# Seven block products for an attention's output projection, with their sums made beside the attention

## The chip, the cores and the metric

One core of a Trainium2 chip runs the kernel. The metric is the device time of one execution in microseconds (us), as the median of several. TensorE (PE, with its weight loads as PEld), VectorE (DVE), ScalarE (ACT), GpSimd (POOL) and SyncE (SP, which here only issues transfers) are the five engines. They are synchronised by semaphores.

## What is computed

A cross-attention layer and a small expert layer, both with residuals, on 8 batches of 100 latent rows of width 1024. Cut to what matters:

```python
k, v = kv @ Wk, kv @ Wv                      # 361 context rows and 100 latent rows per batch
q = rms_norm(layernorm(x) @ Wq); k = rms_norm(k)     # 32 query heads, 8 key heads, width 128
out = softmax(q k^T / sqrt(128)) v           # [8, 100, 4096]
x = x + tanh(g0) * (out @ Wo)                # Wo: 4096 x 1024
x = x + tanh(g1) * experts(layernorm(x))     # router, top 2 of 8, rank 16 each
```

Every float32 matrix product is made of three: each operand is split into a high part (ScalarE copies it to the rounded type) and a low part (VectorE subtracts), and TensorE adds hi*hi, hi*lo and lo*hi.

## The kernel before

The work has four stretches. Keys and values come first (to about 640 us) and are stored to DRAM. Then 64 units run, one for each of 8 key heads g and 8 batches b (u = 8g + b), each with four query heads. Unit u has a slot, written out by hand for each engine (`slot`, L931, L1337, L1714): TensorE makes the scores of the four heads, VectorE takes maxima and forms `nm` (`maxima`, L1678), ScalarE the exponentials, VectorE a reciprocal, GpSimd scales the probabilities (`scale`, L738), and in the following slot TensorE turns them (`turn_probs`, L888), ScalarE and VectorE split them (`p_split`, L1297 and L1671), and TensorE multiplies by the values (`values`, L901). Query projections for later units fill TensorE in between, up to unit 54. ScalarE takes a unit's output from the bank and SP stores it (`store_attn`, L568) to `at_d`. GpSimd makes the reciprocal root mean squares of the queries by a power, four columns for each unit (`unit_rms`, L733); `maxima` waits for them.

The output projection is 32 chunks: for each half of the batches (`th`, four batches, 400 columns), each half of the output columns (`nh`) and each key head g, one chunk of 4 heads x 4 banks x 3 matmuls of 128x400. A product of eight chunks (th, nh) sums in banks 0 to 3. The chunks of the first product fill TensorE in slots 56 to 63 in place of query work (`last_slot`, L981: seven half heads per slot; unit 55 has neither and is the `bare_slot`, L966), and the last one is spread through what follows unit 63. The other 24 follow. Each chunk's 1 MB of weights (`wo_raw`) and 0.8 MB of attention outputs (`at_raw`) come from DRAM when the chunk two before has been split (`load_chunk`, L576), are split by ScalarE (`wo_hi`, `at_hi`: L1332, L1335) and VectorE (`wo_lo`, `at_lo`: L1708, L1712) once TensorE has done with the chunk two before, and at the end of a product VectorE and ScalarE copy two banks each (`accumulators`, L1797, L1411), for which TensorE waits.

The feed-forward part of a batch is five steps on TensorE: `turn_out` (L1026), `turn_y`, `low_rank`, `turn_h`, `up`, with `residual` (L1802), `norm`, `route_top` (L1825), `route_gates` (L1836) and `final` on VectorE, and a power on GpSimd. Batches 0 to 3 have theirs beside the 16 chunks of th = 1, one for every four chunks; batches 4 to 7 after the last chunk.

Of the kernel before, what the change touches and what calls it, by code (L numbers as in the profile page):

```python
# [14 lines left out]
P = 128  # L15
B = 8
# [119 lines left out]

def cols(t):
    return min(P, ROWS_M - t * P)


def build(nc, x, ctxT, Wq, Wkv, Wo, AR, BmT, vecs, rows, out):
    with ExitStack() as ctx:
# [11 lines left out]
        at_d = nc.dram_tensor("at_d", [G, B, P, QW], F32).ap()  # L154

# [81 lines left out]
        xr = at("xr", LO, [P, 2, D])  # L237
        ar = at("ar", AOP, [P, C, AE])
        bm = at("bm", LO + 8 * KB, [P, D])
# [108 lines left out]
        wo_used = sem("wo_used")  # L348
        oT_act = sem("oT_act")
# [73 lines left out]

        def split_after(m):

            return 8 * (m + 1) if m < G else 8 * G + 2 * (m + 1 - G)

        def chunk_of(m):

            return m // (2 * G), m // G % 2, m % G  # L430

        @block.sync
        def _(sp):
# [138 lines left out]
            def load_chunk_weights(m):  # L572
                th, nh, g = chunk_of(m)
                sp.dma_start(wo_raw[:, m % 2], Wo[nh, g]).then_inc(wo_in[m % 2], 16)

            def load_chunk(m):  # L576
                th, nh, g = chunk_of(m)
                k = m % 2
                if m >= 2:
                    sp.wait_ge(wo_lo_done, split_after(m - 2))  # L580
                for i in range(2):
                    sp.wait_ge(ao_stored[i], stored(g * B + th * TB + 2 + i))
                if m >= 2:
                    load_chunk_weights(m)
                sp.dma_start(at_raw[k][:], at_d[g, TB * th:TB * th + TB].rearrange("b p q -> p b q")).then_inc(wo_in[k], 16)
# [10 lines left out]
            load_chunk_weights(0)  # L596
            load_chunk_weights(1)

# [6 lines left out]
            for n in range(AHEAD):  # L605
                load_heads(n)
            for u in range(UNITS):
                load_heads(u + AHEAD)
                if OUT0 + 1 <= u:
                    load_chunk(u - OUT0 + 1)  # L610
                if u >= 1:
                    if u + 1 < UNITS:
                        load_kT(u + 1)
                    store_attn(u - 1)
                    if u + 1 < UNITS:
                        load_vv(u + 1)
                if u in (OUT0 - 4, OUT0 - 3):
                    load_chunk(u - OUT0 + 4)
            load_chunk(G + 2)
            store_attn(UNITS - 1)  # L620

            def load_res(t):
                sp.dma_start(xr[0:NQ, t % 2], x[t]).then_inc(xr_in[t % 2], 16)

            def store(t):
                sp.wait_ge(x2_done, 2 * t + 2)
                sp.dma_start(out[t], x2[0:NQ, t % 2]).then_inc(x2_stored[t % 2], 16)

            for m in range(G + 3, 2 * G):
                load_chunk(m)  # L630
                if m == G + 4:
                    sp.dma_start(ar[:], AR).then_inc(ffn_in, 16)
                    sp.dma_start(bm[:], BmT).then_inc(ffn_in, 16)
                if m == G + 5:
                    load_res(0)
                    load_res(1)
            for c in range(2 * G):
                t = c // 4
                load_chunk(2 * G + c)
                if c % 4 == 0 and t >= 1:  # L640
                    sp.wait_ge(x1_done, 2 * t)
                    load_res(t + 1)
                if c % 4 == 3 and t >= 1:
                    store(t - 1)
# [11 lines left out]
        def _(pool):  # L656
# [86 lines left out]

            unit_rms(0)
            for u in range(UNITS):
                if u + 1 < UNITS:
# [10 lines left out]
        def _(pe):  # L757
# [155 lines left out]
            def chunk_head(m, i, half=None):  # L913

                k = m % 2
                if m < G:
# [3 lines left out]
                if m == 0 and i == 0:  # L920
                    pe.wait_ge(ms_done, 2 * G)
                    pe.wait_ge(pT_lo_done, 4 * OUT0)
                for n in range(4) if half is None else (2 * half, 2 * half + 1):
                    mm = three(ps[n][:, 0:TW].rearrange("p (b q) -> p b q", b=TB),
                               wo_hi[:, k, i, n * P:(n + 1) * P], wo_lo[:, k, i, n * P:(n + 1) * P],
                               at_hi[:, k, :, i * NQ:(i + 1) * NQ], at_lo[:, k, :, i * NQ:(i + 1) * NQ],
                               m % G == 0 and i == 0, m % G == G - 1 and i == R - 1)
# [53 lines left out]
            def last_slot(u):  # L981
# [16 lines left out]
                x_(4)  # L998
                values(u - 1, 2)
                turn_probs(u - 1, 3)  # L1000
                x_(5)
# [13 lines left out]
            def chunk(m, between=None):  # L1015
                for i in range(R):
                    chunk_head(m, i)
                    if between and i == R // 2 - 1:
                        between()

            def accumulators_free(th, nh):
                m = 2 * (2 * th + nh)
                pe.wait_ge(oT_dve, m)
                pe.wait_ge(oT_act, m)

            def turn_out(t):  # L1026
                o = out_bank(t)
                if t == 0:
                    accumulators_free(1, 0)
# [4 lines left out]
                for c in range(C):  # L1034
                    if t == TB and c % 4 == 0:
                        accumulators_free(1 + c // 4, 1 - c // 4)
# [37 lines left out]
            accumulators_free(0, 1)  # L1074
            for m in range(G, 2 * G):
# [857 lines left out]
```

## Time and profile before

| | us |
|---|---|
| median of 3 runs | 1725.62 (1725.24 to 1725.96) |
| the profiled execution | 1723.91 |
| its span | 1722.0 |
| TensorE busy | 1685.8 |
| VectorE, ScalarE, GpSimd busy | 1176.2, 879.9, 719.0 |
| mean granted TensorE clock | 0.996 of full speed |
| moved by the transfers | 278.13 MB, 162 GB/s |

The span runs from the first to the last instruction seen by the profiler. Matmuls overlap: the record of one 128x400 matmul is some 350 ns long, while they start 184 ns apart.

### The profile page before, as it was taken

What the parts mean: (1) busy time and instruction counts of PE and PEld (TensorE: products, weight loads), DVE (VectorE), ACT (ScalarE), POOL (GpSimd) and SP (SyncE); (2) the same over time, 40 slices, a digit from 0 to 9 for tenths busy, and PEclk for the clock granted to TensorE, in tenths of its full rate; (3) what the DMA queues carried; (4) which work ended last, traced back from release to release, by engine and by line L of the source; (5) the groups of instructions that cost most, each with busy time, mean ns of one, the idle gap of its engine ahead of it and who ended that gap; (6) DMA issues with size and microseconds to landing.
All of it is one profiled execution on the core that took longest, in us unless ns stands there. A gap on an engine that the chain in (4) does not pass through costs nothing.

```text
span 1722.0 us, 26303 instructions
## 1 busy us (share of the span) xinstructions
PE 1685.8 (98%) x9312; PEld 1508.0 (88%) x9312; DVE 1176.2 (68%) x2074; ACT 879.9 (51%) x1655; POOL 719.0 (42%) x584
## 2 busy tenths in 40 slices
PE   7999999999999999999999999999999999999996
PEld 6788888678888869999999999999998999999994
DVE  7788877677777743777777777777777774445547
ACT  5455544454544422666666666666666664333321
POOL 1454444224434410666666666666665541000000
PEclk9999999999999999999999999999999999999999
DMA  5567778636556564334444334433454664765532
GB/s 195 161 182 234 236 210 246 166 118 188 159 178 155 142 236 140 104 116 122 133 132 123 122 125 132 123 118 119 131 150 133 211 212 158 260 221 200 194 106 68
DMA packets 215654, 278.13 MB, mean 162 GB/s; under 512 B 51956, under 2 KB 187956, under 8 KB 210020
## 3 DMA queue, kind: packets, MB, share of 16 engines
q1 hardware_dynamic: 214948, 269.90, 50.6%
q10 hardware_dynamic: 576, 6.55, 0.9%
q8 instruction: 75, 1.23, 0.3%
q14 instruction: 55, 0.45, 0.1%
HBM read 189.77 MB, written 86.64 MB: 161 GB/s over the span
## 4 chain that ended last, share of the span: by engine, by line
PE 92%; DVE 3%; ACT 2%; issue 1%; DMA 0%; POOL 0%; SPq 0%; DVEq 0%; ACTq 0%; POOLq 0%
PE bank L759 28%; PE bank L761 27%; PE bank L760 27%; PE bank L897 5%; PE bank L864 2%; PE bank L793 1%; PE bank L1060 1%; ACT w_hi L1124 1%; DMA wr<-Wkv 0%; ACT w_hi L1115 0%; DVE w_lo L1488 0%; PE bank L1071 0%; PE bank L801 0%; PE bank L1072 0%; PE bank L1051 0%
## 5 line engine op out<-in xcount | busy, mean ns | idle before, releaser
L741 POOL TENSOR_SCALAR pr<-pr,rr 100x461 f32<-100x461 f32 x256 | 370.2, 1452 | 293.5 <-DVE rr L1696 293.5
L759 PE MATMUL bank<-w_hi,a_hi 128*128 128x512 f32 (+1 forms) x856 | 340.9, 398 | 11.6 <-DVE a_lo L1471 8.9
L761 PE MATMUL bank<-w_hi,a_lo 128*128 128x512 f32 (+1 forms) x856 | 334.9, 391 | 0.0
L760 PE MATMUL bank<-w_lo,a_hi 128*128 128x512 f32 (+1 forms) x856 | 334.4, 391 | 0.0
L1308 ACT ACTIVATE pr<-bank,nm,rq 100x461 f32<-100x461 f32 x256 | 188.7, 737 | 155.8 <-DVE nm L1687 152.7
L1681 DVE TENSOR_REDUCE mx<-bank 100x1 f32<-100x461 f32 x256 | 161.4, 631 | 80.3 <-PE bank L761 75.3
L759 PEld LDWEIGHTS bank<-w_hi,a_hi 128*128 128x128 f32 (+1 forms) x856 | 157.8, 184 | 48.7 <-issue 10.0
L761 PEld LDWEIGHTS bank<-w_hi,a_lo 128*128 128x128 f32 (+1 forms) x856 | 157.7, 184 | 38.2
L759 PE MATMUL bank<-xT_hi,wq_hi 128*128 128x400 f32 x512 | 188.2, 367 | 0.4 <-issue 0.4
L760 PEld LDWEIGHTS bank<-w_lo,a_hi 128*128 128x128 f32 (+1 forms) x856 | 158.0, 185 | 34.8
L759 PE MATMUL bank<-at_hi,wo_hi 128*128 128x400 f32 x512 | 182.6, 357 | 2.8 <-DVE oT L1800 2.8
L761 PE MATMUL bank<-xT_hi,wq_lo 128*128 128x400 f32 x512 | 178.0, 348 | 0.0
L760 PE MATMUL bank<-at_lo,wo_hi 128*128 128x400 f32 x512 | 178.0, 348 | 0.0
L760 PE MATMUL bank<-xT_lo,wq_hi 128*128 128x400 f32 x512 | 177.9, 347 | 0.0
L761 PE MATMUL bank<-at_hi,wo_lo 128*128 128x400 f32 x512 | 177.9, 347 | 0.0
L697 POOL TENSOR_TENSOR msk<-ssk,epst 128x4 f32<-128x4 f32 (+1 forms) x60 | 22.9, 382 | 348.7 <-DVE ssk L1502 348.7
L1299 ACT ACTIVATE pT_hi<-bank 120x400 fp32r<-120x400 f32 (+2 forms) x256 | 127.5, 498 | 58.7 <-PE bank L897 58.5
L1675 DVE TENSOR_TENSOR pT_lo<-bank,pT_hi 120x400 fp32r<-120x400 f32 (+2 forms) x256 | 144.6, 565 | 9.5 <-ACT pT_hi L1299 8.7
L897 PEld LDWEIGHTS bank<-ident,pr 100*120 100x120 f32 (+2 forms) x1024 | 110.1, 148 | 12.4
L1471 DVE TENSOR_TENSOR a_lo<-st,a_hi 128x512 fp32r<-128x512 f32 (+1 forms) x104 | 92.5, 891 | 35.3 <-ACT a_hi L1101 34.8
L897 PE MATMUL bank<-ident,pr 100*120 100x100 f32 (+2 forms) x1024 | 116.4, 253 | 0.0
L752 POOL TENSOR_SCALAR mv<-mv 100x1 f32<-100x1 f32 x8 | 9.7, 1214 | 255.2 <-DVE mv L1815 255.2
(133 smaller groups left out, 3497.7 us busy)
## 6 DMA issues: line engine op xcount, KB each, us to landing
wo_raw<-Wo SPq DMA_DIRECT2D x32, 1024.0 KB, 4.9
kT_d<-kst SPq DMA_DIRECT2D x56, 512.0 KB, 5.4
v_d<-vst SPq DMA_DIRECT2D x56, 512.0 KB
at_raw<-at_d SPq DMA_DIRECT2D x32, 800.0 KB, 7.1
kT<-kT_d SPq DMA_DIRECT2D x64, 361.0 KB, 4.7
kvr<-ctxT SPq DMA_DIRECT2D x44, 512.0 KB, 5.6
wq_raw<-Wq SPq DMA_DIRECT2D x32, 512.0 KB, 5.9
vv<-v_d SPq DMA_DIRECT2D x64, 240.0 KB
```

Source lines behind the costliest of these rows:

```text
L697: pool.tensor_tensor(msk[0:n, m], ssk[0:n, m], epst[0:n], ALU.add).then_inc(msk_done, 1)
L741: pool.tensor_scalar(pr[0:NQ, u % 2, i], pr[0:NQ, u % 2, i], rr[0:NQ, i:i + 1], None, ALU.mult).then_inc(p_done, 1)
L759: pe.matmul(o, lh, rh, start=start, stop=False, skip_group_check=more)
L760: pe.matmul(o, lh, rl, start=False, stop=False, skip_group_check=more)
L761: return pe.matmul(o, ll, rh, start=False, stop=stop, skip_group_check=more)
L864: mm = pe.matmul(o, sq[:, n % 2, bb * NQ:(bb + 1) * NQ], ones[:], start=True, stop=True)
L897: mm = pe.transpose(ps[ptbank(u, t)][0:ROWS[t], i * NQ:(i + 1) * NQ], pr[0:NQ, u % 2, i, OFF[t]:OFF[t] + ROWS[t]], ident[0:NQ, 0:NQ])
L1299: act.activation(pT_hi[0:ROWS[t], t], ps[ptbank(u, t)][0:ROWS[t], 0:QW], ACT.Copy).then_inc(pT_hi_done, 1)
L1308: act.activation(pr[0:NQ, u % 2, i], ps[BS[i % 2]][0:NQ, 0:NK], ACT.Exp, bias=nm[0:NQ, i:i + 1], scale=rq[0:NQ, g, R * b + i:R * b + i + 1 ...
L1471: dve.tensor_tensor(a_lo[:, i % RING, :, 0:n], a_src(i), a_hi[:, i % RING, :, 0:n], ALU.subtract).then_inc(a_lo_done, 1)
L1675: dve.tensor_tensor(pT_lo[0:ROWS[t], t], ps[ptbank(u, t)][0:ROWS[t], 0:QW], pT_hi[0:ROWS[t], t], ALU.subtract).then_inc(pT_lo_done, 1)
L1681: dve.tensor_reduce(mx[0:NQ, i:i + 1], ps[BS[i % 2]][0:NQ, 0:NK], AX.X, ALU.max).then_inc(mx_done, 1)
```

## The change

The projection is done as a Winograd form of Strassen's scheme: rows (batches 0 to 3, 4 to 7), inner dimension (key heads 0 to 3, 4 to 7) and output columns (two halves of 512) are each cut in two, and seven products of a quarter of the inner sums take the place of eight. A product now is four chunks (GQ = 4), 28 in all.

- **Operands.** Three products take plain blocks of the heads (P1, P2, P4) and three plain blocks of the weights (P1, P2, P3); the rest take sums of blocks. Four sums of weights are made on GpSimd beside the units and stored to a DRAM tensor `wt_d`: 16 steps, each a load of four 128x512 blocks (1 MB), four additions and a store (1 MB). S3, the difference of the batch halves for key heads 0 to 3, is made the same way in 16 steps in slots 34 to 51 (`s3_d`). S1, S2 and S4 are made of whole chunks' heads on GpSimd just before the split, four 128x400 additions each, for P5, P6 and P3; S2 is stored (`s2_d`) and loaded again for P3, which takes 2.6 MB per chunk.
- **Order.** P1, P7, then P5 and P6 chunk by chunk in turn, P4, P2, P3. P5 and P4 sum in banks 4 to 7, the others in 0 to 3. P1 and P7 are the chunks beside units 56 to 63. The two copies each of VectorE and ScalarE at the end of P1 are made within slot 60.
- **Results.** The products are added up by VectorE while it empties the banks (four instructions for P6, P4 and P3, two for P2) and by three 128x1600 and one 128x800 additions on GpSimd.
- **Feed-forward.** The batches 4 to 7 come first: their steps stand beside the last 8 chunks (P2, P3), one batch for every two chunks; batch 3's in that order has its routing and two last steps behind the last chunk. Then come the other four.
- **Power.** `unit_rms` makes one power of 16 columns for four units, ahead of the scales of each unit u with u % 4 = 3.
- **SP's order.** The load of the next unit's keys stands first in a slot; transfers of the sums follow, then chunks, the store of the unit before and the values' loads. The chunks' first weights are loaded in slots 53 and 54.

```diff
+CHUNKS = ([(P1, c) for c in range(GQ)] + [(P7, c) for c in range(GQ)] + [(o, c) for c in range(GQ) for o in (P5, P6)] +
+          [(o, c) for o in (P4, P2, P3) for c in range(GQ)])
+WT_OPS = ((2, 3, 2, True), (0, 2, 0, False), (3, 3, 0, True), (1, 1, 0, True))
+WT_STEPS = GQ * R
+for _n in range(4 * WT_STEPS):
+    WT_AT.setdefault(max(-1, (_n - 4) * 6 // 7), []).append(_n)
+S3_AT = 34
+for _t in range(B // 2):
+    for _i, _a in enumerate((0, 2, 3, 4, 5)):
+        FFN_AT.setdefault(4 * _t + _a, []).append((_i, _t))
...
@@ sync
             for n in range(AHEAD):
                 load_heads(n)
+                if n == AHEAD - 2:
+                    load_t(0)
+                    load_t(1)
             for u in range(UNITS):
                 load_heads(u + AHEAD)
+                if 1 <= u < UNITS - 1:
+                    load_kT(u + 1)
+                for n in range(WT_STEPS):
+                    if u == WT_DONE[n] + 1:
+                        store_t(n)
+                    if u == WT_DONE[n] + 2 and n + 2 < WT_STEPS:
+                        load_t(n + 2)
+                if 0 <= u - S3_AT - 2 < S3_STEPS:
+                    store_s3(u - S3_AT - 2)
+                if 0 <= u - S3_AT < S3_STEPS:
+                    load_s3(u - S3_AT)
...
@@ gpsimd
             def unit_rms(u):
                 g, b = u // B, u % B
                 pool.wait_ge(ms_done, 2 * g + b // TB + 1)
-                pool.tensor_tensor(rq[0:NQ, g, R * b:R * b + R], ms[0:NQ, R * b:R * b + R], mhalf[0:NQ, 0:R], ALU.pow).then_inc(rq_done, 1)
+                c = slice(R * b, R * (b + TB))
+                pool.tensor_tensor(rq[0:NQ, g, c], ms[0:NQ, c], mhalf[0:NQ, 0:R * TB], ALU.pow).then_inc(rq_done, 1)
...
+            def chunk_sums(m):
+                o, c = CHUNKS[m]
+                pool.wait_ge(at_in[m % 4], a_loaded(m))
+                if o == P6:
+                    pool.wait_ge(at_sum, summed(m - 1))
+                to, x, y = {P5: (a21[c % 2], a21[c % 2], a22[c % 2]), P6: (a11[c % 2], a21[c % 2], a11[c % 2]),
+                            P3: (at_raw[m % 2], at_raw[m % 2], at_more[:, m % 2])}[o]
+                for b in range(TB):
+                    pool.tensor_tensor(to[:, b], x[:, b], y[:, b], ALU.add if o == P5 else ALU.subtract).then_inc(at_sum, 1)
             unit_rms(0)
+            for i in WT_AT[-1]:
+                weight_sum(i)
             for u in range(UNITS):
-                if u + 1 < UNITS:
+                if u % TB == TB - 1 and u + 1 < UNITS:
                     unit_rms(u + 1)
                 for i in range(R):
                     scale(u, i)
+                for i in WT_AT.get(u, ()):
+                    weight_sum(i)
+                if 0 <= u - S3_AT - 1 < S3_STEPS:
+                    early_sum(u - S3_AT - 1)
+                if u == UNITS - 2:
+                    chunk_sums(FIRST_OF[P5])
+            for m in range(FIRST_OF[P6], LAST_OF[P6] + 1):
+                chunk_sums(m)
+            first, second = (slice(0, C // 2), slice(C // 2, C))
+            pool.wait_ge(oT_dve, 10)
+            pool.wait_ge(oT_act, 6)
+            pool.tensor_tensor(oT_late[:, first], oT_late[:, first], oT_early[:, second], ALU.add).then_inc(mix_done, 1)
+            pool.tensor_tensor(oT_early[:, second], oT_early[:, second], oT_late[:, second], ALU.add).then_inc(mix_done, 1)
+            pool.wait_ge(mix_done, 2)
+            pool.tensor_tensor(oT_late[:, second], oT_late[:, second], oT_late[:, first], ALU.add).then_inc(mix_done, 1)
             for t in range(B):
+                if t == 2:
+                    chunk_sums(FIRST_OF[P3])
+                    chunk_sums(FIRST_OF[P3] + 1)
+                    pool.wait_ge(oT_act, 8)
+                    pool.tensor_tensor(oT_early[:, 2:4], oT_early[:, 2:4], c_tmp[:], ALU.add).then_inc(mix_done, 1)
+                if t == 3:
+                    chunk_sums(FIRST_OF[P3] + 2)
+                    chunk_sums(FIRST_OF[P3] + 3)
...
@@ tensor
+            stages = (turn_out, turn_y, low_rank, turn_h, up)
+            for n in range(4 * GQ):
+                for i in range(2):
+                    chunk_head(TAIL0 + n // 2, n % 2 * 2 + i)
+                for i, t in sorted(FFN_AT.get(n, ())):
+                    stages[i](t)
...
@@ vector
+            def accumulators(o):
+                dve.wait_ge(wo_used, R * (LAST_OF[o] + 1))
+                bank = 4 * (o in UPPER)
+                if o == P6:
+                    dve.wait_ge(oT_act, 2)
+                if o in (P4, P3):
+                    dve.wait_ge(mix_done, 3)
+                for n in (0, 1) if o in (P1, P7, P5, P2) else range(4):
+                    acc = ps[bank + n][:, 0:TW]
...
+                    dve.tensor_tensor(to, acc, oT_early[:, n] if o == P6 else to, ALU.add).then_inc(oT_dve, 1)
...
+            accumulators(P3)
             a, b, c, d = range(TB, B)
-            for do, t in ((residual, a), (final, a - 1), (norm, a), (residual, b), (residual, c), (norm, b), (route, a),
+            for do, t in ((route_top, a - 1), (residual, a), (route_gates, a - 1), (norm, a), (residual, b), (final, a - 1),
+                          (residual, c), (norm, b), (route, a),
```

## Rows read from the trace of the kernel before

**Rows 1.** The page, parts 1 (busy us, share, instructions) and 4 (chain by engine).
```profile
PE 1685.8 (98%) x9312; PEld 1508.0 (88%) x9312; DVE 1176.2 (68%) x2074; ACT 879.9 (51%) x1655; POOL 719.0 (42%) x584
...
PE 92%; DVE 3%; ACT 2%; issue 1%; DMA 0%; POOL 0%; SPq 0%; DVEq 0%; ACTq 0%; POOLq 0%
```

**Rows 2.** Windows: from:to, us, busy PE PEld DVE ACT POOL, PEclk, DMA share, GB/s.
```profile
1315.00:1325.00 10.00, 8.62 (x33) 7.73 (x34) 8.14 (x20) 7.90 (x19) 4.36 (x4) 0.66 0.47 150
1446.00:1518.00 72.00, 71.41 (x387) 70.67 (x386) 33.27 (x18) 27.95 (x19) 0.00 (x0) 1.00 0.64 226
1683.00:1722.00 39.00, 25.30 (x144) 17.70 (x143) 29.13 (x86) 5.56 (x16) 3.41 (x8) 0.92 0.25 75
```

**Rows 3.** Windows: one slot of the attention.
```profile
901.37:912.74 11.37, 11.37 (x74) 10.81 (x73) 8.70 (x20) 7.49 (x16) 7.54 (x5) 1.00 0.36 109
```

**Rows 4.** Timeline of PE: first and last matmul of the second product (384).
```profile
1447.14 0.45 PE L759 MATMUL bank<-at_hi,wo_hi 128*128 128x400 f32 x1 [0.59 <-DVE oT L1800]
...
1517.67 0.34 PE L761 MATMUL bank<-at_hi,wo_lo 128*128 128x400 f32 x1
```

**Rows 5.** Waits of PE: total us, times, longest.
```profile
PE bank L759 <- DVE oT L1800: 2.8, 3, 1.1
```

**Rows 6.** Timelines of DVE and PE in the slot of unit 60.
```profile
1387.96 0.16 DVE L1696 RECIPROCAL rr<-rs 100x1 f32<-100x1 f32 x1 [0.41 <-ACT pr L1308]
...
1388.54 0.43 PE L759 MATMUL bank<-at_hi,wo_hi 128*128 128x400 f32 x1
```

**Rows 7.** Groups by line and form: busy us, mean ns, idle before, releaser.
```profile
L736 POOL TENSOR_TENSOR rq<-ms,mhalf 100x4 f32<-100x4 f32 x64 | 88.0, 1375 | 44.1 <-DVE ms L1645 44.1
...
L1708 DVE TENSOR_TENSOR wo_lo<-wo_raw,wo_hi 128x2048 fp32r<-128x2048 f32 x24 | 54.8, 2282 | 60.3 <-ACT wo_hi L1332 60.3
...
L1712 DVE TENSOR_TENSOR at_lo<-at_raw,at_hi 128x1600 fp32r<-128x1600 f32 x24 | 43.6, 1818 | 0.0
...
L707 POOL TENSOR_TENSOR rstd<-rstd,mhalf 100x1 f32<-100x1 f32 x8 | 4.4, 555 | 0.7
```

**Rows 8.** Timelines of POOL and DVE in the keys' stretch.
```profile
48.91 3.39 POOL L673 TENSOR_TENSOR st<-kvr 128x512 f32<-128x512 f32 x1
...
72.98 1.29 POOL L673 TENSOR_TENSOR st<-kvr 128x512 f32<-128x512 f32 x1
...
73.04 1.77 DVE L1509 TENSOR_TENSOR kn<-cb,rk 128x512 f32<-128x512 f32 x1 [1.48 <-POOL rk L701]
```

**Rows 9.** Timelines of DVE, PE and POOL in a slot.
```profile
899.37 0.16 DVE L1687 SCALAR_TENSOR_TENSOR nm<-mx,rq 100x1 f32<-100x1 f32 x1
899.53 0.57 DVE L1675 TENSOR_TENSOR pT_lo<-bank,pT_hi 121x400 fp32r<-121x400 f32 x1
...
900.90 0.35 PE L759 MATMUL bank<-pT_hi,vv 121*128 121x400 f32 x1
...
908.35 1.83 POOL L736 TENSOR_TENSOR rq<-ms,mhalf 100x4 f32<-100x4 f32 x1
```

**Rows 10.** Timelines of POOL and PE in the first two slots.
```profile
681.53 2.47 POOL L736 TENSOR_TENSOR rq<-ms,mhalf 100x4 f32<-100x4 f32 x2 [44.12 <-DVE ms L1645]
687.20 4.30 POOL L741 TENSOR_SCALAR pr<-pr,rr 100x461 f32<-100x461 f32 x3 [3.21 <-DVE rr L1696]
...
693.72 0.91 PE L897 MATMUL bank<-ident,pr 100*121 100x100 f32 x8
```

**Rows 11.** The page, part 6: transfers, count, KB each, median us to landing.
```profile
wo_raw<-Wo SPq DMA_DIRECT2D x32, 1024.0 KB, 4.9
```

**Rows 12.** Timeline of DVE: copies of a product and the next chunk's last split.
```profile
1518.06 1.06 DVE L1800 COPY oT<-bank 128x400 f32<-128x400 f32 x2 [2.79 <-PE bank L761]
...
1522.99 1.82 DVE L1712 TENSOR_TENSOR at_lo<-at_raw,at_hi 128x1600 fp32r<-128x1600 f32 x1
```

**Rows 13.** Timeline of DVE: first and last instruction of a batch's routing.
```profile
1549.41 0.17 DVE L1827 TENSOR_TENSOR lg<-bank,rowc 100x8 f32<-100x8 f32 x1 [5.37 <-PE bank L1060]
...
1553.73 0.29 DVE L1854 TENSOR_TENSOR hw<-bank,we 100x128 f32<-100x128 f32 x1
```

More of the change, by code:

```diff
@@ L348, in build @@
         wo_used = sem("wo_used")
+        t_in = [sem("t_in0"), sem("t_in1")]
+        t_sum = sem("t_sum")
+        t_stored = [sem("t_stored0"), sem("t_stored1")]
+        at_sum = sem("at_sum")
+        at_in = [sem(f"at_in{i}") for i in range(4)]
+        s3_in = [sem(f"s3_in{i}") for i in range(4)]
+        s3_sum = sem("s3_sum")
+        s3_stored = [sem(f"s3_stored{i}") for i in range(4)]
+        s2_stored = sem("s2_stored")
+        mix_done = sem("mix_done")
         oT_act = sem("oT_act")
@@ L422, in experts_bank, with a_raw, a_loaded, summed @@
             return (2, 6, 4, 0)[t - TB] if t >= TB else 6
+        def a_raw(m):
+            o, c = CHUNKS[m]
+            return a21[c % 2] if o == P5 else a11[c % 2] if o == P6 else at_raw[m % 2][:]
         def split_after(m):
             return 8 * (m + 1) if m < G else 8 * G + 2 * (m + 1 - G)
-        def chunk_of(m):
-            return m // (2 * G), m // G % 2, m % G
+        def a_loaded(m):
+            return 16 * sum(A_LOADS[CHUNKS[n][0]] for n in range(m % 4, m + 1, 4))
+        def summed(m):
+            return R * sum(o in SUMMED for o, c in CHUNKS[:m + 1])
+        def batch_of(t):
+            return (t + TB) % B
         @block.sync
@@ new lines, in load_chunk, with load_s3, store_s3 @@
+            def load_chunk(m):
+                load_weights(m)
+                load_heads_of(m)
+            def load_s3(n):
+                if n >= 4:
+                    sp.wait_ge(s3_stored[n % 4], 16 * (n // 4))
+                for th in range(2):
+                    u = n // TB * B + th * TB + n % TB
+                    sp.wait_ge(ao_stored[u % 2], stored(u))
+                    sp.dma_start(s3b[n % 4][th], at_d[u // B, u % B]).then_inc(s3_in[n % 4], 16)
+            def store_s3(n):
+                sp.wait_ge(s3_sum, n + 1)
+                sp.dma_start(s3_d[n // TB, :, n % TB], s3b[n % 4][0]).then_inc(s3_stored[n % 4], 16)
@@ new lines, in store_s2, with load_t, store_t @@
+            def store_s2(c):
+                sp.wait_ge(at_sum, summed(FIRST_OF[P6] + 2 * c))
+                sp.dma_start(s2_d[c], a11[c % 2]).then_inc(s2_stored, 16)
+            def load_t(n):
+                if n >= 2:
+                    sp.wait_ge(t_stored[n % 2], 16 * (n // 2))
+                sp.dma_start(tb[:, n % 2], Wo.rearrange("n (k c) p r d -> c r p (n k) d", k=2)[n // R, n % R]).then_inc(t_in[n % 2], 16)
+            def store_t(n):
+                sp.wait_ge(t_sum, 4 * n + 4)
+                sp.dma_start(wt_d.rearrange("t c p r d -> c r p t d")[n // R, n % R], tb[:, n % 2]).then_inc(t_stored[n % 2], 16)
@@ L997, in last_slot @@
                 x_(3)
-                x_(4)
+                swap = PARTS * (u - OUT0 - 1) + 4 == 2 * R * FIRST_OF[P7]
+                if not swap:
+                    x_(4)
                 values(u - 1, 2)
                 turn_probs(u - 1, 3)
+                if swap:
+                    x_(4)
                 x_(5)
@@ L1013, in _, with chunk @@
                 values(UNITS - 1, t)
-            def chunk(m, between=None):
+            def chunk(m):
                 for i in range(R):
                     chunk_head(m, i)
[L1018 to L1024, printed above, removed]
             def turn_out(t):
@@ L1894, in route @@
-            def route(t):
-                route_top(t)
-                route_gates(t)
+            accumulators(P4)
+            for n in range(4 * GQ):
+                m = TAIL0 + n // 2 + 1
+                at_last = FFN_AT.get(n - 1, ())
+                if n == 2 * GQ:
+                    accumulators(P2)
+                for i, t in at_last:
+                    if i == 2:
+                        route(t)
+                    if i == 4:
+                        final(t)
+                for i, t in FFN_AT.get(n - 2, ()):
+                    if i == 0:
+                        norm(t)
+                if m < len(CHUNKS):
+                    (chunk_heads if n % 2 else chunk_weights)(m)
+                for i, t in at_last:
+                    if i == 0:
+                        residual(t)
```

319 lines of the change are left out of this document (208 added, 111 removed).

## The prediction

> **What bounds the kernel now.** I read the page's busy times and the chain that ended last first: TensorE is busy 1685.8 of 1722.0 us and the chain runs through it for 92% [rows 1]. So a matmul taken out is worth its full pitch, unless its going uncovers a wait. Next the stretches: the output projection alone (8 chunks, 1446 to 1518 us) has TensorE busy 71.4 of 72 us with VectorE at 33, ScalarE at 28, GpSimd at 0 and 226 GB/s; the closing 39 us, the second half of the feed-forward part, are the one place where TensorE is not full (25.3) and VectorE is (29.1) [rows 2]. In the attention a slot (one unit: scores, softmax, values, and query work between) takes 11.37 us, all of it TensorE; GpSimd is busy 7.5, VectorE 8.7 [rows 3]. So there is room beside TensorE for the additions, and the question is whose turn they come in at.
>
> **Products removed.** 32 chunks become 28, of 48 matmuls each: 192 fewer. From the first matmul of a free projection stretch to its last are 383 pitches in 70.53 us, 0.184 each [rows 4]. 192 x 0.184 = 35.4 us off, all on the path. What the products need besides (splits) shrinks by the same 4 chunks and is hidden.
>
> **Turns of the banks.** Before, three products end with TensorE waiting for their copies, 2.8 us in all [rows 5]. After, P5 and P4 use the upper banks, P6 and P4 cover the copies of P7, P5 and P6, and at P2 to P3 the low-rank matmuls of one batch cover them. 2.8 us off (bounds 0 and 4: each wait also restarts the pipeline). New is P1 to P7 inside slot 60. The four copies come behind the unit's last exponential and reciprocal. That reciprocal is at 1387.96 in a slot of this kind, two copies of 0.57 then end near 1389.2, and the half head that would have followed on TensorE at 1388.54 [rows 6] comes behind the delayed one, near 1390.4: 1.9 us on (0.9 to 3).
>
> **Weights' sums and S3 in the slots.** 64 additions of 128x512 and 16 of 128x400 go to GpSimd, four of the 64 ahead of slot 0, the others one per slot and two in every sixth; from slot 35 to 50 one S3 addition more. An unhindered 128x512 addition takes 1.29 us, so a 128x400 one 1.0. The powers shrink from 64 to 16, one before each four units; a one-column power takes 0.56 and a four-column one 1.38 on the mean [rows 7], so a 16-column one is put at 3 to 5. GpSimd's load per slot goes from 7.5 to 8.1, at most 10 or so, of 11.37: there is room. What costs is order. A GpSimd addition and a VectorE instruction with two SBUF inputs exclude each other: the addition from 72.98 to 74.27 holds the VectorE product begun at 73.04 to 74.81, 1.77 instead of 0.69 us; and an addition begun at 48.91 under a weight split is 3.39 long [rows 8]. The trace agrees here with the Trainium skill, SBUF — State Buffer, Who interferes with whom: the pair of ports is locked for a whole instruction, which speaks against this change's additions. In a slot GpSimd falls free at 908.35 [rows 9]; one addition ends at 909.6, two at 910.9, one behind a query-weight split at 910.5. The small product nm, two SBUF inputs, comes 11.37 after 899.37, at 910.74. Behind it VectorE makes pT_lo, ready at 900.08, for the values at 900.90: 0.85 us of slack [rows 9]. nm is held only where an addition runs at 910.74: the 9 slots with two weights' additions and the 8 odd ones with one and S3's, up to 1.1 us, so at most 0.3 is lost in each. The long power, every fourth slot, can hold the same nm, or the next scales. No row shows the two together; I take half of 17 x 0.3, 2.5 us, since most of the wait fits the slack; bounds 0 and 15 (51 slots x 0.3).
>
> **The first slot.** The power starts at 681.53, the first scale at 687.20 (1.43 each), and the fourth ends just before TensorE's first transposes start, 693.72 [rows 10]. The power (3 us) and four additions (5.2) end near 689.7, so four scales end near 695.5: 1.8 us on (0 to 3).
>
> **Transfers.** Each partial sum is a load and a store of 1 MB, 32 MB in 51 slots, S3 9.6 MB in 16 slots: up to 110 GB/s on top of the 109 of [rows 3]. A weights' chunk lands in 4.9 us [rows 11], and the chip's queue moved 226 GB/s over 72 us without a wait [rows 2]. SP sends the keys ahead of them and the values behind, each with a slot to land. In the last stretch P5 and P6 want 16 MB in 70 us, P3 2.6 MB per chunk of 10 us. Nothing on the path; without that cover a late chunk is TensorE's wait (a rival).
>
> **Sums of heads.** 12 chunks (P5, P6, P3) get four 128x400 additions each on GpSimd, 4.2 us, against 8.8 us of matmuls per chunk. A chunk's split before: the chunk two back ends at 1518.06, and the last of the split ends at 1524.8 [rows 12], 6.7 later, 6.1 without ScalarE's copies ahead of it. w_lo (2.29) and at_lo (1.82) [rows 7] may each wait for one addition, 1.0: 8.1, under 8.8. Covered, thinly. The first P5 chunk is split among the last unit's splits: 0.7 us (0 to 3). P3's sums stand in GpSimd's order behind each batch's square root, which waits for a residual on VectorE; worked through they come 1 us early. I take 0.5 (0 to 5).
>
> **The mixing additions.** Three of 128x1600 start when P6 is added in. By 1.29 x 1600/512 each holds 4.0 us. Counting from the end of P6: VectorE's four adds to 2.3, w_lo to 4.6, mix 1 to 8.6, at_lo to 10.3 where the next chunk was due at 8.8; mix 2 to 14.3, w_lo to 16.4, mix 3 to 20.4, at_lo to 22.1 against 19.2. 1.6 + 2.9 = 4.5 us on (0 to 7; nothing if a long addition lets go in between, or if the order falls better). By the rule of the Trainium skill named above the whole 4.5 stands; if the ports were let go within the addition the sum would be 1698.5.
>
> **The end.** Behind the last product stand four adds on VectorE (2.3) where there were two copies (1.1), and batch 3's routing, which VectorE did before the last product's end: top and gates 0.85 + 1.65 = 2.5 [rows 13]. The closing stretch is VectorE's (29 of 39 us), so both are paid: 3.7, with the waits about 3.8 (2 to 6).
>
> **Sum.** -35.4 - 2.8 + 1.9 + 2.5 + 1.8 + 0.7 + 0.5 + 4.5 + 3.8 = -22.5. The profiled execution took 1723.9 (span 1722.0): 1701.4. It lies 1.7 under the median of the runs, 1725.6: 1703.
>
> **Rivals.**
> - All additions hidden (VectorE and GpSimd happen to alternate well): only the swap and the end cost, -35.4 - 2.8 + 1.9 + 3.8 = -32.5, 1693. For it: the slack everywhere computed; against it: the lock rows. 0.13.
> - The last stretch is short of time: if each of the 12 summed chunks comes 1 us late beyond the 0.5, 11.5 on: 1714.5. For it: 8.1 of 8.8 us, and transfers of 2.6 MB. 0.15.
> - The clock falls. In the bare slot TensorE's waits near 1 us are followed by 0.50 of full speed, 1.2 GHz, for some 6 us; 1315 to 1325 shows 0.66 on the mean, so 3.2 us lost [rows 2]. Two such falls, behind the mix waits and the swap: +6.4, 1709. Against it: the present bank waits of 1.1 us leave the clock at 1.00 in 1446 to 1518. The Trainium skill, TensorE: Matmul & The Clock Gate, What's actually happening, has the clock released by activity and throttled without it; waits of 1 to 3 us do bear on it. 0.05.
> - Slower or no gain: the additions hold nm in all 51 slots [rows 8, 9]. If the additions start later than I place them, nm waits for one whole addition, 1.15 us, and another two-input instruction of the slot (q_lo, before the next scores) for the next: 2 x 1.15 less the slack of 0.85 is 1.45 us, x 51 = 74 in place of 2.5: 1774.5. It decides from 0.49 us per slot on (25/51). Against it: GpSimd falls free 2.4 us before nm. 0.05.
> - The work isn't less (some product is made of more matmuls than I count): the lists give 28 x 48. 0.02, time as before.
>
> **How the numbers follow.** The forecast (1697 to 1709) has 0.60. The range reaches to the hidden case and the late chunks, 1693 to 1714, and leaves out the last two. A measurement of this kernel tells 0.2%, 3.5 us, from no change. Faster: all but the slower rival and the unchanged one, 0.93; same 0.03; slower 0.04.
>
> **What would show it.** 1344 projection matmuls instead of 1536, at 0.184. Slots of 11.37 us on the mean over 0 to 50, or 11.4 to 11.45 by my term, and nm longer than 0.16 us there. TensorE waiting for at_lo twice in P4, 1 to 3 us; for the copies once in slot 60. 45 us from the last product's end to the end of the span instead of 41. Wrong would be: slots of 11.8 and more, waits for at_sum through ScalarE in P5, P6 or P3, a clock under 0.95 outside the bare slot, or no wait at all in P4.

## The result, and the profile after

The changed kernel takes 1716.8 us (median of 4 runs, 1715.7 to 1719.9) against 1725.8 (4 runs, 1725.2 to 1729.3): ratio 0.9948, 95% interval 0.9936 to 0.9960. It is 9.0 us faster where 22.5 were forecast; 1703 was predicted, 1693 to 1714 the range. The profiled execution took 1715.65, its span 1713.8.

The page after, parts 1 and 4 (before: [rows 1]), and groups of the attention's slots, on VectorE from 697 to 1290 us and on GpSimd from 697 to 1265 us (line, shapes, count, busy us, mean ns, idle before):

```profile
PE 1665.8 (97%) x9120; PEld 1475.3 (86%) x9120; DVE 1239.6 (72%) x2078; ACT 865.1 (50%) x1647; POOL 873.9 (51%) x668
...
PE 70%; DVE 18%; issue 4%; ACT 4%; DMA 2%; POOL 0%; DVEq 0%; SPq 0%; ACTq 0%; POOLq 0%
...
L1897 DVE TENSOR_TENSOR q_lo<-q_raw,q_hi 128x400 fp32r<-128x400 f32 x50 | 80.2, 1604 | 12.0 <-ACT q_hi L1519 12.0
L1805 DVE TENSOR_TENSOR wq_lo<-wq_raw,wq_hi 128x1024 fp32r<-128x1024 f32 x25 | 57.7, 2307 | 0.0
...
L912 POOL TENSOR_TENSOR tb<-tb 128x512 f32<-128x512 f32 x58 | 84.0, 1450 | 0.4
L896 POOL TENSOR_TENSOR rq<-ms,mhalf 100x16 f32<-100x16 f32 x12 | 35.2, 2931 | 0.0
```

TensorE has lost 192 matmuls, as announced, but only 20.0 us of busy time where 35.4 were counted. Slots 2 to 50, with the same 3529 matmuls, count as 567.7 us busy where they were 557.1: the records of neighbouring matmuls overlap and cover most of a short wait. The chain of work, which before ran through VectorE for 3%, now does so for 18%, 10 of them by maxima, wq_lo and q_lo. These two splits are the rows to look at: before the change the same groups read

```profile
L1655 DVE TENSOR_TENSOR q_lo<-q_raw,q_hi 128x400 fp32r<-128x400 f32 x52 | 46.8, 901 | 12.6 <-ACT q_hi L1288 12.6
L1563 DVE TENSOR_TENSOR wq_lo<-wq_raw,wq_hi 128x1024 fp32r<-128x1024 f32 x26 | 31.8, 1225 | 1.3
```

so each q_lo has grown by 0.7 us and each wq_lo by 1.1. The end of an odd slot (unit 17) and the start of the next show how, by the timelines of GpSimd, VectorE and TensorE after:

```profile
893.63 1.44 POOL L901 TENSOR_SCALAR pr<-pr,rr 100x461 f32<-100x461 f32 x1 [0.62 <-DVE rr L1938]
895.04 1.49 POOL L912 TENSOR_TENSOR tb<-tb 128x512 f32<-128x512 f32 x1
...
893.80 1.58 DVE L1897 TENSOR_TENSOR q_lo<-q_raw,q_hi 128x400 fp32r<-128x400 f32 x1 [0.26 <-ACT q_hi L1519]
895.31 2.31 DVE L1805 TENSOR_TENSOR wq_lo<-wq_raw,wq_hi 128x1024 fp32r<-128x1024 f32 x1
897.54 0.62 DVE L1923 TENSOR_REDUCE mx<-bank 100x1 f32<-100x461 f32 x1
898.29 0.16 DVE L1929 SCALAR_TENSOR_TENSOR nm<-mx,rq 100x1 f32<-100x1 f32 x1
898.40 0.57 DVE L1917 TENSOR_TENSOR pT_lo<-bank,pT_hi 121x400 fp32r<-121x400 f32 x1
...
899.03 0.45 PE L973 MATMUL bank<-pT_hi,vv 121*128 121x400 f32 x1
```

The addition stands behind the fourth scale, q_lo and wq_lo run beside the two, and wq_lo ends only at 897.62. The maxima of unit 18, whose first scores began at 895.80, start right behind it, 1.74 later; in slot 17 and before the change they start 0.82 to 0.85 after the first scores. nm, pT_lo and the values follow late. TensorE pays for it twice in slot 18: 0.19 us at the values' first matmul (899.03 above), and the rest of the 0.47 in the transposes behind the third head's scores, the fifth of which starts at 900.89, when the next pT_lo has just ended (900.85). These eight transposes after and, in the slot of before that is shown below:

```profile
900.31 1.14 PE L1111 MATMUL bank<-ident,pr 100*120 100x100 f32 x8
...
890.71 0.85 PE L897 MATMUL bank<-ident,pr 100*120 100x100 f32 x8
```

Before the change, VectorE had 0.68 us in hand at that place, and wq_lo and q_lo now want 1.8 more:

```profile
885.32 1.23 DVE L1563 TENSOR_TENSOR wq_lo<-wq_raw,wq_hi 128x1024 fp32r<-128x1024 f32 x1
887.22 0.64 DVE L1681 TENSOR_REDUCE mx<-bank 100x1 f32<-100x461 f32 x1 [0.68 <-PE bank L761]
```
In the slots that end without a wq_lo (here unit 16) VectorE still waits after the change for TensorE:

```profile
882.44 1.58 DVE L1897 TENSOR_TENSOR q_lo<-q_raw,q_hi 128x400 fp32r<-128x400 f32 x1 [0.27 <-ACT q_hi L1519]
885.28 0.64 DVE L1923 TENSOR_REDUCE mx<-bank 100x1 f32<-100x461 f32 x1 [1.26 <-PE bank L975]
```

The windows show the outcome for units 17 and 18 (from:to, us, busy PE PEld DVE ACT POOL, PEclk, DMA share, GB/s), and those of the closing stretch from the last product's last matmul on at the bottom, first after and then before:

```profile
884.43:895.80 11.37, 11.37 (x73) 10.78 (x72) 8.57 (x19) 7.50 (x16) 7.21 (x6) 1.00 0.63 195
895.80:907.62 11.82, 11.74 (x73) 10.71 (x72) 9.67 (x19) 6.44 (x15) 7.10 (x6) 1.00 0.75 230
...
1667.45:1713.80 46.35, 30.66 (x170) 23.13 (x168) 33.44 (x103) 6.12 (x18) 3.46 (x8) 0.87 0.22 63
```
```profile
1681.05:1722.00 40.95, 26.62 (x154) 18.78 (x152) 30.18 (x88) 6.60 (x19) 3.41 (x8) 0.93 0.24 71
```

Taken from the starts of each unit's first scores in both traces, the span's 8.2 us come apart like this: 0.6 on ahead of slot 0 (not the change: that start moves between 684.3 and 687.6 in the runs below), slots 0 and 1 4.7 on, slots 2 to 50 14.4 on (0.45 to 0.6 in most even slots, 0.7 to 0.8 in slots 8, 32, 40, 44 and 46; of the odd slots 0.8 in slot 43, 0.08 in 7 and 31, nothing in the others), slots 51 to 59 0.1, slots 60 to 62 1.5 on, and from slot 63 to the end 29.4 off.

In slots 0 and 1 the TensorE clock has a part. TensorE waits 2.79 us ahead of slot 1's first scores at 695.64 (0.76 at 693.04 before the change), and within this wait, at 694.75, the granted clock falls to 0.50 of full speed, the lower level of 1.2 GHz, until 701.57. Before the change it stays at 1.00 there. The windows after and before:

```profile
694.00:702.00 8.00, 6.36 (x23) 5.81 (x24) 4.90 (x9) 2.02 (x5) 4.56 (x5) 0.57 0.75 207
...
694.00:702.00 8.00, 8.00 (x55) 7.56 (x55) 6.34 (x16) 5.11 (x13) 4.62 (x4) 1.00 0.00 0
```

### The profile page after: what moved, and what is told of

Read it like the earlier page. It is cut to its first block, busy times and chain, and to the rows that moved or that the text cites. A ratio compares the mean times of both kernels' runs of the same rounds, so it can differ in the third digit from the quotient of the medians.

```text
span 1713.8 us, 26112 instructions
## 1 busy us (share of the span) xinstructions
PE 1665.8 (97%) x9120; PEld 1475.3 (86%) x9120; DVE 1239.6 (72%) x2078; ACT 865.1 (50%) x1647; POOL 873.9 (51%) x668
## 4 chain that ended last, share of the span: by engine, by line
PE 70%; DVE 18%; issue 4%; ACT 4%; DMA 2%; POOL 0%; DVEq 0%; SPq 0%; ACTq 0%; POOLq 0%
PE bank L973 21%; PE bank L975 20%; PE bank L974 20%; DVE mx L1923 4%; PE bank L1111 3%; DVE wq_lo L1805 3%; DVE q_lo L1897 3%; PE bank L1078 2%; DVE pT_lo L1917 2%; DMA kT_d<-kst 1%; PE bank L1007 1%; ACT pr L1539 1%; DVE q_raw L1875 1%; DVE nm L1929 1%; DVE wo_lo L1943 1%
## 5 line engine op out<-in xcount | busy, mean ns | idle before, releaser
L973 PE MATMUL bank<-at_hi,wo_hi 128*128 128x400 f32 x448 | 159.9, 357 | 2.9 <-DVE at_lo L1954 2.5
L974 PE MATMUL bank<-at_lo,wo_hi 128*128 128x400 f32 x448 | 155.7, 347 | 0.0
L975 PE MATMUL bank<-at_hi,wo_lo 128*128 128x400 f32 x448 | 155.6, 347 | 0.0
L1111 PE MATMUL bank<-ident,pr 100*120 100x100 f32 (+2 forms) x1024 | 122.3, 255 | 2.3 <-DVE pT_lo L1917 0.4
L1332 ACT ACTIVATE a_hi<-st 128x512 fp32r<-128x512 f32 (+1 forms) x104 | 63.2, 609 | 83.8 <-PE bank L975 73.6
```

The lines of the kernel that those rows point to most:

```text
L973: pe.matmul(o, lh, rh, start=start, stop=False, skip_group_check=more)
L974: pe.matmul(o, lh, rl, start=False, stop=False, skip_group_check=more)
L975: return pe.matmul(o, ll, rh, start=False, stop=stop, skip_group_check=more)
L1111: mm = pe.transpose(ps[ptbank(u, t)][0:ROWS[t], i * NQ:(i + 1) * NQ], pr[0:NQ, u % 2, i, OFF[t]:OFF[t] + ROWS[t]], ident[0:NQ, 0:NQ])
L1332: act.activation(a_hi[:, i % RING, :, 0:cols(k % NT)], a_src(i), ACT.Copy).then_inc(a_hi_done, 1)
```

## The experiments

**My theory:** the additions cost what they do because of where they stand, beside VectorE's q_lo and wq_lo. **The rivals:** their transfers (42 MB beside the slots), their mere amount, and the 16-column powers. Every ratio is against the kernel before; "slots 0-1" and "2-50" are us over before, from the same starts.

| run | median us | ratio, 95% interval | slots 0-1 | slots 2-50 |
|---|---|---|---|---|
| after | 1716.8 | 0.9948 (0.9936-0.9960) | 4.7 | 14.4 |
| e1_one_column | 1699.4 | 0.9841 (0.9823-0.9858) | 0.0 | 0.0 |
| e2_behind_nm | 1709.3 | 0.9901 (0.9884-0.9917) | 0.7 | 9.2 |
| e3_odd_moved | 1704.3 | 0.9865 (0.9848-0.9881) | 3.6 | 1.0 |
| e3b_even_moved | 1722.7 | 0.9978 (0.9968-0.9988) | 3.6 | 19.9 |
| e4_power_per_unit | 1712.8 | 0.9921 (0.9905-0.9938) | 1.7 | 12.4 |
| e5_none_ahead | 1700.4 | 0.9846 (0.9830-0.9863) | 0.8 | 1.1 |
| e6_mix_quarters | 1696.3 | 0.9828 (0.9812-0.9844) | 0.8 | 1.0 |
| e7_mix_column | 1697.8 | 0.9831 (0.9815-0.9848) | 0.8 | 1.1 |
| e8_behind_q_lo | 1703.3 | 0.9862 (0.9846-0.9879) | 3.3 | 1.9 |
| e9_residual_before_final | 1697.3 | 0.9832 (0.9815-0.9848) | 0.8 | 1.1 |
| e10_from_slot_1 | 1696.3 | 0.9831 (0.9813-0.9849) | 0.0 | 0.1 |

**1. Additions of one column**, so that the sums stay unfinished.
```diff
-                pool.tensor_tensor(tb[:, n % 2, to], tb[:, n % 2, a], tb[:, n % 2, b],
+                pool.tensor_tensor(tb[:, n % 2, to, 0:1], tb[:, n % 2, a, 0:1], tb[:, n % 2, b, 0:1],
```
and early_sum alike.

> The 64 weights' additions and the 16 early additions of S3 work on one column instead of 512 or 400; all their waits and all 42 MB of their transfers stay, so the products P7, P5, P6 and P4 come out of unfinished sums. Theory (an addition queued directly behind the fourth scale holds q_lo, 1.58 instead of 0.90 us, and wq_lo, 2.31 instead of 1.22, and the next slot's first maxima come late): q_lo back to 0.90, wq_lo to 1.22, slots 2 to 50 back to 11.37 on the mean (-14 us), the first two slots nearly back (-4): 1697 to 1700 against 1716. Rival (the transfers beside the slots delay loads or slow SBUF): no change, 1714 to 1718, q_lo and wq_lo as long as now.

1699.4. q_lo and wq_lo are back to 901 and 1225 ns, and every slot up to 50 has its old length:

```profile
L1897 DVE TENSOR_TENSOR q_lo<-q_raw,q_hi 128x400 fp32r<-128x400 f32 x50 | 45.1, 901 | 12.1 <-ACT q_hi L1519 12.1
L1805 DVE TENSOR_TENSOR wq_lo<-wq_raw,wq_hi 128x1024 fp32r<-128x1024 f32 x25 | 30.6, 1225 | 1.2
```

All transfers and all the long powers are still there. So the transfers beside the slots cost nothing there, and neither do the powers by themselves.

**2. All additions behind a slot's first nm.** The pool's loop, with END_AT empty here, GAP_AT spreading the 64 over slots 0 to 50:
```diff
-            for i in WT_AT[-1]:
-                weight_sum(i)
...
+                if u in GAP_AT or u in S3_GAP:
+                    pool.wait_ge(nm_done, 4 * u + 1)
+                for i in GAP_AT.get(u, ()):
+                    weight_sum(i)
+                for n in S3_GAP.get(u, ()):
+                    early_sum(n)
                 for i in range(R):
                     scale(u, i)
```

> Full additions, but each stands in GpSimd's order in front of a slot's first scale, behind a wait for the slot's first nm, where GpSimd idles for 3.2 us (885.2 to 888.35) and VectorE reads banks; at most two per slot, none ahead of slot 0. Theory: q_lo and wq_lo are free again, slots 2 to 50 take 11.37 to 11.45, and the first slots are shorter: 1697 to 1703. In the slots with two additions the first scale comes up to 0.8 us late, which I expect to be hidden. Rival (it is the amount of additions, wherever they stand, or their transfers): 1712 to 1717, with nm, pT_lo or q_raw longer instead.

1709.3, a miss against 1697 to 1703. q_lo is back at 0.90, and from slot 2 on the slots with one addition behind nm have their old length; but those with two are 0.13 to 0.6 longer. The timelines of GpSimd and VectorE in such a slot:

```profile
893.16 2.65 POOL L915 TENSOR_TENSOR tb<-tb 128x512 f32<-128x512 f32 x2 [2.57 <-DVE nm L1938]
...
894.84 0.99 DVE L1938 SCALAR_TENSOR_TENSOR nm<-mx,rq 100x1 f32<-100x1 f32 x1
```

The second addition holds the second nm, 0.99 instead of 0.16, and the exponentials wait. My expectation had the late scale in it and not this. So there is room for one addition there, not for two.

**3. Only one parity moved.** In the run e3_odd_moved the additions at the ends of odd slots went behind the next nm, in its mirror those at the ends of even slots:
```diff
+    _u = max(-1, (_n - 4) * 6 // 7)
+    _move = _u % 2 == 1 and _u > 0
+    (GAP_AT if _move else END_AT).setdefault(_u + _move, []).append(_n)
```

> Only the additions behind the last scale of the odd slots (those in which wq_lo is made) move behind the next slot's first nm; those of the even slots and the four ahead of slot 0 stay. Theory (the loss is wq_lo's, 0.47 us in each even slot because VectorE has 1.26 us of slack at the other slots' ends): nearly all 14 us of slots 2 to 50 come back, 1701 to 1705, with q_lo still 1.58 in the even slots. Rival (every held q_lo costs its share): half of it, 1708 to 1711.

> The mirror of the run that moved the odd slots' additions: now those behind the last scale of the even slots move behind the next slot's first nm, and those beside wq_lo in the odd slots stay. Theory (the loss is wq_lo's alone): the even slots keep their 0.47 us, nothing is gained, and the slots with two additions behind nm lose 0.4 more: 1716 to 1722. Rival (every addition behind a fourth scale costs a share): 1709 to 1712.

1704.3 and 1722.7. Moving the odd half gives back 13.4 of the 14.4 us, with q_lo still held in the even slots (mean 1242 over all). Moving the even half gives nothing and costs 5.5, in the odd slots that now have two additions behind nm; I had allowed for less of this, and the time lies just above my 1716 to 1722. An addition beside q_lo alone is free, since VectorE waits 1.26 us for TensorE behind it; two cost at most 0.08 (slots 7 and 31). Three, at the end of slot 42, with a 16-column power behind them, cost 0.8 in slot 43: GpSimd is done with them only at 1192.87, makes its four scales without a pause until 1198.58, and q_lo beside them takes 2.58 us. Beside wq_lo even one addition costs 0.47.

**4. A power per unit.**
```diff
-                if u % TB == TB - 1 and u + 1 < UNITS:
+                if u + 1 < UNITS:
                     unit_rms(u + 1)
```
with four columns each, and VectorE's waits for rq_done as before the change.

> One four-column power per unit as before the change, instead of one of 16 columns for four units; all else is as after. Theory (the 2.9 us power is hidden, since the slots with it are no longer than the others): the first slot gains up to 1.5 us from the shorter first power, the rest stays or loses where the power, now 1 to 1.5 us in every slot behind the addition, runs at the first nm: 1714 to 1722. Rival (the long power is what makes slots late): 1705 to 1711.

1712.8, between the two: 3.1 us come from slots 0 and 1 (I had allowed 1.5), 2.0 from slots 2 to 50. Together with e1_one_column, where the long powers cost nothing, the long power is harmless by itself and costs something where additions are queued with it. The traces tell where: the 2.0 us are those of slots 7 and 8, 31 and 32, 43 and 44, and 0.15 in slot 40. In slots 7, 31 and 43 the 16-column power stands directly behind two or three additions; it does so in slot 19 too, and there costs nothing.

**5. No additions ahead of slot 0** (on top of e3_odd_moved): `_u = _n * 4 // 5`.

> As the run that moved the odd slots' additions, and no weights' addition ahead of slot 0: the 64 stand evenly in slots 0 to 50. Theory (the four additions, 5.2 us, push the first four scales and with them everything in slots 0 and 1): slots 0 and 1 take 9.0 and 11.4 instead of 11.0 and 13.0 us, 3.6 off, 1700 to 1702. Rival (the 16-column power of 2.9 us is what delays the first slot): less than 1 us off, 1703 to 1705.

1700.4, in the range of the theory; but slots 0 and 1 gain 2.8, not 3.6: they take 9.7 and 11.6 us and still lose 0.8. Not all of the 2.8 is the scales' delay. TensorE's clock was granted at 0.50 for 3.4 us of slot 1 in e3_odd_moved (13.0 us) and for 6.8 us in the changed kernel (14.1 us), and stayed at 1.00 in e5_none_ahead (11.6 us). These runs do not separate the clock's part from the rest.

**6. The mixing additions** in quarters and, in another run, of one column (both on top of e5_none_ahead):
```diff
-            pool.tensor_tensor(oT_late[:, first], oT_late[:, first], oT_early[:, second], ALU.add).then_inc(mix_done, 1)
+            for n in range(4):
+                pool.tensor_tensor(oT_late[:, n], oT_late[:, n], oT_early[:, 4 + n], ALU.add).then_inc(mix_done, 1)
```

> As the run without additions ahead of slot 0, and the three mixing additions of 128x1600 are twelve of 128x400. Theory (VectorE's splits of the P4 chunks wait for whatever GpSimd addition runs, so for one quarter at most where it was a whole one): TensorE's two waits for at_lo in P4, 2.9 us together, fall to 0 to 1.5: 1.5 to 2.9 less than that run. Rival (a queue of short additions holds VectorE just as a long one): the waits stay within 0.5 us of 2.9.

> As the run without additions ahead of slot 0, but the three mixing additions work on one column of each 400, so that the last products are added to unfinished sums. Theory: both waits for at_lo in P4 are gone, 2.9 us less than that run. Rival (P4's waits come from its loads or from the four adds of P6 on VectorE): at least 1 us of them is left.

1696.3 with quarters and 1697.8 with one column, where the mixed sums stay unfinished, against 1700.4: 2.7 us less without the mixing, and as much or more with it in quarters. In both, TensorE no longer waits for at_lo in P4. First after, then with quarters: VectorE's split of a P4 chunk and GpSimd's first mixing sum beside it.

```profile
1542.66 5.24 DVE L1954 TENSOR_TENSOR at_lo<-at_raw,at_hi 128x1600 fp32r<-128x1600 f32 x1
...
1540.55 5.68 POOL L951 TENSOR_TENSOR oT_late<-oT_late,oT_early 128x1600 f32<-128x1600 f32 x1 [19.75 <-DVE oT_early L1971]
...
1547.96 0.46 PE L973 MATMUL bank<-at_hi,wo_hi 128*128 128x400 f32 x1 [0.72 <-DVE at_lo L1954]
...
1558.78 0.45 PE L973 MATMUL bank<-at_hi,wo_hi 128*128 128x400 f32 x1 [1.73 <-DVE at_lo L1954]
```
```profile
1525.98 2.67 DVE L1969 TENSOR_TENSOR at_lo<-at_raw,at_hi 128x1600 fp32r<-128x1600 f32 x1
...
1523.86 7.70 POOL L964 TENSOR_TENSOR oT_late<-oT_late,oT_early 128x400 f32<-128x400 f32 x4 [19.75 <-DVE oT_early L1986]
```

The split waits for one quarter (2.67 instead of 1.82) and not for a whole addition (5.24). GpSimd is slower for it, 7.7 instead of 5.7 us, and has the time.

**7. Additions behind q_lo**, on the changed kernel, and nothing else moved:
```diff
+                if (u in WT_AT or 0 <= u - S3_AT - 1 < S3_STEPS) and u + 1 < UNITS:
+                    pool.wait_ge(q_lo_done, u + 2)
                 for i in WT_AT.get(u, ()):
                     weight_sum(i)
```

> On the changed kernel as it is: GpSimd's additions wait, behind the fourth scale, until VectorE has made the next q_lo. In the even slots this moves them by a fraction of a us, in the odd ones wq_lo begins where the wait ends. Theory (the pair of instructions is served in the order in which they begin: q_lo of 0.90 ends at 894.70, before the scale does at 895.07, and wq_lo then begins first): q_lo 0.90, wq_lo 1.2 to 1.3, the addition longer, slots 2 to 50 near 11.37: 1702 to 1706. Rival (a queued addition takes the turn however it stands): q_lo 0.90 but wq_lo 2.3, with the next maxima 0.7 us earlier than now, so most of the 0.47 is back anyway, 1705 to 1709. Third (nothing but the place matters): 1716.

1703.3: one wait gives back 13.5 us, 12.5 of them in slots 2 to 50. What it leaves there is mostly in slots 37 (0.67) and 46 (0.43), the cause of which is open. VectorE and GpSimd at the end of the odd slot 17:

```profile
889.47 0.90 DVE L1899 TENSOR_TENSOR q_lo<-q_raw,q_hi 128x400 fp32r<-128x400 f32 x1 [0.26 <-ACT q_hi L1521]
890.42 1.23 DVE L1807 TENSOR_TENSOR wq_lo<-wq_raw,wq_hi 128x1024 fp32r<-128x1024 f32 x1
892.32 0.64 DVE L1925 TENSOR_REDUCE mx<-bank 100x1 f32<-100x461 f32 x1 [0.68 <-PE bank L977]
...
889.30 1.44 POOL L901 TENSOR_SCALAR pr<-pr,rr 100x461 f32<-100x461 f32 x1 [0.60 <-DVE rr L1940]
890.71 2.08 POOL L912 TENSOR_TENSOR tb<-tb 128x512 f32<-128x512 f32 x1
```

wq_lo begins before the addition and has its 1.23; now it is the addition that is long, 2.08 instead of 1.29, where nobody waits for it. That is the rule of the Trainium skill, SBUF — State Buffer, Who interferes with whom, that the order of issue decides which of the two blocks; this trace agrees, 2.31 and 1.49 us in one order, 1.23 and 2.08 in the other.

**8. The closing stretch** (on top of e6_mix_quarters): residual(c) ahead of final(a - 1) in VectorE's order.

> As the run with the mixing in quarters, but in the closing stretch VectorE makes the residual of batch 6 before it finishes batch 3, where it waited 1.63 us for TensorE. Theory (the closing stretch is VectorE's, each idle us of it is paid at the end): 1.0 to 1.6 off, 1694.7 to 1695.3 against 1696.3. Rival (the end hangs on the chain of the last batch through all engines): within 0.5 of it.

1697.3, no gain: the last product's end stands 47.4 us before the end of the span (46.9 without the edit, and 45.6 in e10_from_slot_1, whose order there is that of e6_mix_quarters). So no gain shows, and these three differ by more than the 1.0 to 1.6 I had hoped for. What sets the end is open.

**9. Nothing in slot 0, S3 alone behind nm in odd slots** (on top of e6_mix_quarters):
```diff
+_order = [u for u in range(1, 51) for _ in range(1 + (u % 2 == 0 and u // 2 * 14 // 25 > (u // 2 - 1) * 14 // 25))]
```

> As the run with the mixing in quarters, but the weights' additions begin at the end of slot 1 and S3's even ones stand alone behind the first nm of odd slots instead of second in even ones. Theory (slot 0's end has no slack for the two additions, 0.85 us in slots 0 and 1; two additions behind one nm cost 0.13 in eight slots): 1.9 off, 1694 to 1695. Rival (the 0.66 us in slot 0 is the 16-column power's): 1.0 to 1.2 off, slot 0 still 9.6.

In the trace it does what it should: slots 0 and 1 take 9.0 and 11.4, their old lengths, and slots 2 to 50 are only 0.1 over before in all. The median, 1696.3, is that of e6_mix_quarters, with runs from 1693.1 to 1699.8; 1.9 us is less than these tell apart. With quarters and either placing, the kernel stands about 30 us under the one before.

## Why the prediction was wrong

Its own sum, -22.5, against -8.2 in the profiled executions. Of the 14.3 us between them 11.9 are the first term here.

- **Slots 2 to 50: +2.5 predicted, +14.4 measured. This is the step that failed.** It asked only whether nm is held. q_lo, which VectorE makes beside the fourth scale, is in no term (only the rival of 1774.5 names it), and wq_lo is taken to go first: "one behind a query-weight split at 910.5" lets the addition wait for wq_lo. The runs show the other order: with an addition queued behind the fourth scale q_lo takes 1.58 instead of 0.90, so wq_lo begins behind the addition (895.31 against 895.04) and takes 2.31 instead of 1.23. In e8_behind_q_lo, with q_lo at 0.90, the order is the predicted one, and slots 2 to 50 lose 1.9. The trace of before would have told that in every other slot VectorE has only 0.68 us in hand between wq_lo and the next maxima. It could not tell that q_lo would be held: a four-column power follows the fourth scale there, and every q_lo beside it takes 0.90. What the term did ask came much as worked out: in the eight slots behind two additions (7, 13, 19 and so on to 49) the first nm took 0.47 to 0.60 instead of 0.16, and those slots, 43 aside, took 11.37 to 11.47. The slack of 0.85 is 0.82 by [rows 9]. The bounds, 0 and 15, held the value; the range of the sum did not.
- **Slots 0 and 1: +1.8 predicted, +4.7 measured.** The four scales ended at 695.9, close to the 695.5 worked out. Left out were the third and fourth nm beside additions (0.97 and 0.45), at the end of slot 0 a q_lo of 1.93 beside the last scales with two additions queued behind them, and the fall of the clock to 0.50 behind TensorE's wait of 2.79 us. Moving the additions of the odd slots gives 1.2 back, taking the four sums away 2.8, the two at the end of slot 0 the last 0.8.
- **Mix: +4.5 predicted, 2.45 of waits in the trace, 2.7 by the run without.** The mechanism is right: the order of sums and splits is the predicted one, each at_lo ended only after the sum that it met, and both waits came, at the two chunks named, as 0.72 and 1.73 where 1.6 and 2.9 stood. The size of a sum was wrong. The records of 5.2 to 5.7 us hold the sum's own waits for splits; from the end of at_lo at 1547.90 to its own end at 1551.41 the second took 3.5 us, and so did the other two, where 4.0 was put. (The chain is also added up short: 4.6, 4.0 and 1.82 make 10.4, 14.3 and 2.29 make 16.6, and with exact steps the sum comes to 4.9, not 4.5.)
- **End: +3.8 predicted, +5.4 measured** (46.35 against 40.95). VectorE's busy time there grew by 3.3 (33.44 against 30.18), near the 3.7 counted. The rest stands beside idle time of VectorE, 3.0 instead of 1.4 us for the experts' banks, and a granted clock of 0.87 instead of 0.93; how much each costs was not tested.
- **Products, bank turns, P5's start, P3's sums: -35.4 - 2.8 + 0.7 + 0.5 = -37.0 predicted.** From slot 63 to the end 29.4 came off; with 2.5 for the mix and 5.4 for the end that is -37.3. Chunks 8 to 15, with their sums on GpSimd, took 8.83 each: thin cover, but cover. The rival of late chunks (1714.5) came near the measured time by luck: no such chunk was late.
- **Swap: +1.9 predicted, +1.8** in slot 60 (15.97 instead of 14.21).
- **The powers: 3 to 5 predicted, 2.9 measured**, at no cost by themselves; with a power of four columns for each unit the slots 0 to 50 were 5.1 us shorter, 2.0 of them in slots 2 to 50.
- **The clock, a rival at 0.05.** A new fall came in slots 0 and 1, and longer ones than before in the closing stretch, but none at the swap or behind the waits of the mix, where the rival had put them. And 3.2 us for such a fall is not what the bare slot shows: it takes 17.32 us before, with the clock at 0.50 for 6.8 us of it, and 17.28 to 17.33 in six runs in which the clock did not fall there.

The rival "slower by held two-input instructions" had the right mechanism for q_lo, but put it at every slot and at 1.45 us; it is 0.47 in every second one. "Wrong would be: slots of 11.8 and more" is what the even slots show.

## What to carry to other kernels

Before work goes to GpSimd, list every VectorE instruction with two SBUF inputs that runs in the window, not only the one next on the critical path, and add the hold to each until it meets a wait for another engine. Ask also what stands directly behind the GpSimd instruction that it meets. Idle time of GpSimd in a slot is no room by itself: here the additions cost 14.4 us in slots 2 to 50 behind the fourth scale, 1.9 with one wait for q_lo ahead of them, and 0.1 when spread. Where the two engines must meet, put the short or urgent one first and cut the long one in pieces of the size of the slack.

## What the runs showed of the hardware that I had not expected

- What is queued behind a GpSimd instruction counts too. q_lo begun 0.17 us into a scale takes 0.90 when nothing stands behind the scale (slots 51 to 53), or a 16-column power (slot 54), an addition of one column, or an addition kept back by a wait; begun 1.12 us into a scale (slots 56 to 62) it takes 0.57. It takes 1.58 when a full addition is queued directly behind the scale, although that addition's own record begins only at 895.04, when q_lo of 0.90 would long have ended. So the scale alone seems to let VectorE go after about 0.5 us of its 1.44 (0.17 + 0.90 - 0.57, an estimate), and with a full addition behind it after about 1.2. Why is not settled.
- The same pair costs one side or the other by the order of their beginnings: wq_lo 2.31 with the addition 1.49, or 1.23 with 2.08.
- A 16-column power takes 2.9 us where four of four columns took 1.0 to 2.0 each; as a single piece it is cheaper, and as an obstacle longer.
